# Latent attention of a decoder block: fp32 scores in row tiles of 32, in units of four heads and half the queries

## The reference, cut to what matters

```python
q = (x @ Wq.T).reshape(b, t, 16, 16).transpose(0, 2, 1, 3)
latent = layernorm(x @ Wdkv.T, ln_g, ln_b)
k = (latent @ Wuk.T).reshape(b, t, 16, 16).transpose(0, 2, 1, 3)
v = (latent @ Wuv.T).reshape(b, t, 16, 16).transpose(0, 2, 1, 3)
q = apply_rope(q); k = apply_rope(k)
scores = jnp.einsum('bhqd,bhkd->bhqk', q, k) / np.sqrt(16)
scores = jnp.where(causal, scores, -jnp.inf)
attn = jax.nn.softmax(scores, axis=-1)
out = jnp.einsum('bhqk,bhkd->bhqd', attn, v)
```

## Time and profile before

| | |
|---|---|
| median of 3 runs | 2898.22 us (2896.65 to 2900.44) |
| profiled execution | 2899.45 us, its span 2897.6 us |
| PE busy | 2651.6 us, 92% |
| DVE busy | 1506.8 us, 52% |
| ACT busy | 1233.8 us, 43% |
| POOL busy | 337.4 us, 12% |
| mean granted TensorE clock | 0.967 |

### The profile page before, as it was taken

How to read it: one execution, slowest core, us unless ns; L and a number is a source line. 1 busy time by engine, 2 the same in 40 slices (tenths; PEclk the granted TensorE clock), 3 DMA queues, 4 the chain that set the end, 5 groups by cost and what they waited for, 6 DMA issues and landing times.

```text
span 2897.6 us, 43591 instructions
## 1 busy us (share of the span) xinstructions
PE 2651.6 (92%) x14862; PEld 1626.2 (56%) x14863; DVE 1506.8 (52%) x3738; ACT 1233.8 (43%) x2620; POOL 337.4 (12%) x561
## 2 busy tenths in 40 slices
PE   7999997999999997999999987989999988987998
PEld 4565654445656544445656544445556554446997
DVE  3434468754333568744333568743443568743443
ACT  3444225653443325654443325644442425641221
POOL 1000013012000013012000022012000022013111
PEclk9999999999999999999999999999999999998999
DMA  2000000001000000001000000001000000032111
GB/s 93 12 12 1 15 1 1 1 13 41 12 11 1 15 1 1 1 13 41 17 6 1 15 1 1 0 13 46 12 6 1 15 1 1 0 124 87 55 54 39
DMA packets 32394, 56.38 MB, mean 19 GB/s; under 512 B 7108, under 2 KB 23570, under 8 KB 31858
## 3 DMA queue, kind: packets, MB, share of 16 engines
q1 hardware_dynamic: 27490, 41.33, 4.5%
q0 software_dynamic: 4752, 13.02, 1.2%
HBM read 40.01 MB, written 14.32 MB: 19 GB/s over the span
## 4 chain that ended last, share of the span: by engine, by line
PE 77%; DVE 12%; ACT 5%; issue 3%; POOL 2%; DMA 0%; SPq 0%; DVEq 0%; ACTq 0%; POOLq 0%
PE ps L939 9%; PE ps L911 8%; PE ps L884 8%; PE ps L869 5%; PE ps L929 5%; PE ps L1168 4%; PE ps L1258 4%; PE ps L1153 4%; PE ps L1272 4%; PE ps L894 4%; DVE arena L1526 3%; PE ps L1128 3%; PE ps L1031 3%; PE ps L824 3%; PE ps L1049 2%
## 5 line engine op out<-in xcount | busy, mean ns | idle before, releaser
L1360 DVE TENSOR_REDUCE neg_max<-ps 128x1 f32<-128x128 f32 (+7 forms) x256 | 194.0, 758 | 567.6 <-PE ps L914 567.3
L1526 DVE TENSOR_REDUCE arena<-ps 128x1 f32<-128x512 f32 (+3 forms) x768 | 376.4, 549 | 109.3 <-PE ps L1131 51.9
L774 ACT ACTIVATE arena<-ps 128x512 f32<-128x512 f32 (+3 forms) x768 | 320.3, 513 | 157.4 <-PE ps L1156 152.5
L939 PE MATMUL ps<-arena 128*128 128x512 f32 (+3 forms) x768 | 318.0, 501 | 4.6 <-ACT arena L660 0.5
L660 ACT ACTIVATE arena<-ps 128x512 f32<-128x512 f32 (+3 forms) x384 | 188.2, 490 | 295.3 <-PE ps L929 293.2
L1128 PE MATMUL ps<-arena 128*128 (+4 forms) x768 | 249.2, 335 | 52.1 <-DVE arena L1526 50.2
L911 PE MATMUL ps<-arena 128*128 128x512 f32 (+3 forms) x768 | 290.7, 490 | 4.4 <-ACT arena L669 4.4
L1153 PE MATMUL ps<-arena 128*128 (+4 forms) x768 | 245.0, 329 | 11.9 <-ACT arena L759 2.8
L884 PE MATMUL ps<-turned_t,arena 128*128 128x512 f32 x512 | 228.8, 600 | 1.1 <-ACT turned_t L631 1.1
L911 PEld LDWEIGHTS ps<-arena 128*128 128x128 f32 x768 | 139.1, 190 | 135.3 <-issue 114.8
L929 PE MATMUL ps<-ident,arena 128*128 128x128 f32 x1152 | 193.0, 278 | 20.8 <-ACT arena L648 11.4
(11 more groups left out here) (231 smaller groups left out, 4246.8 us busy)
## 6 DMA issues: line engine op xcount, KB each, us to landing
arena<-in_w_qkv SPq DMA_DIRECT2D x32, 384.0 KB, 3.1
arena<-in_w SPq DMA_DIRECT2D x2, 4096.0 KB, 16.8
xin<-in_x SPq DMA_DIRECT2D x5, 1024.0 KB, 5.2
xres_ids<-sorted_res SPq DMA_DIRECT2D x35, 129.0 KB, 2.1
xin<-sorted_rows SPq DMA_DIRECT2D x35, 128.0 KB, 2.0
w_out<-in_w_out SPq DMA_DIRECT2D x1, 1024.0 KB
out<-xin,out_row POOLq DMA_INDIRECT x35, 2.7
sorted_res<-xin SPq DMA_DIRECT2D x4, 129.0 KB, 2.2
```

The lines of the kernel that those rows point to most:

```text
L774: nc.scalar.activation(mprobs_t[kb % 2][:, j, lo:hi], ps[:, 3 + use % 3, 0:hi - lo], ACT.Exp).then_inc(mexp_done, 1)
L939: nc.tensor.matmul(ps[:, 6 + g, lo:BANK], v_rows[par][:, kb, :], probs_t[u % 4][:, lo:BANK], start=(kb == 0), stop=True, skip_group_check= ...
L1360: nc.vector.tensor_reduce(neg_max[:, par, t:t + 1], ps[:, buf:buf + 2, :].rearrange("p a n -> p (a n)")[:, 0:n], AX.X, ALU.max, negate=Tru ...
L1526: nc.vector.tensor_reduce(max_part[:, j, t, c:c + 1], ps[:, u % 3, 0:n], AX.X, ALU.max).then_inc(ms_taken, 1)
```

## The change

It replaces everything from the turned stacks to the products.

- q and k stay fp32. The rope writes them into `q_slots` and `k_slots`, 32 numbers per head: number 0 is 0 for a query and -1 for a key, 1 to 16 are the values, the rest 0. GpSimd fills the constants by five memsets. TensorE turns four heads at once (`turn_slots`, 8 uses of 4 transposes for q, before the latents are turned, and 8 for k), ScalarE stores all 16 halves. No stacks are made, and the keep-warm matmuls of the stage are gone.
- A score is one fp32 matmul of 32 rows of the contraction: head j of a group lies in partitions 32 j to 32 j + 31 (row tiles). No matmul adds a mask.
- The maximum of a chunk on the diagonal is taken by one VectorE instruction that adds the mask and reduces (`tensor_tensor_reduce`), 128 of 192 chunks of a batch; the others keep `tensor_reduce`. The maximum goes into slot number 0, is turned (fp32), and VectorE adds it into `q_heads_t` (`take_max`).
- ScalarE takes the exponentials of two heads in one instruction. GpSimd sets the part above the diagonal to zero afterwards (`affine_select`, 32 a batch), and products of diagonal items wait for it. Values are read from `mv_rows` directly. There are four buffers of exponentials of half the queries each.
- The work of a batch is 8 units of (group of heads, half of the queries), in the order `UNITS`; a unit of the first half has 4 items (key tiles) and 16 chunks of maxima, one of the second half 8 items and 32 chunks. While the items of a unit run, the chunks of the next are issued, 6 ahead, evenly over the items. The first unit's chunks use 7 banks, the others 3.
- The statistics for the next batch are taken on VectorE in the middle (after `take_max(5)`), the normalised rows after the last maximum. SyncE waits for `mout_taken` where it waited for `vg_ready`.

```diff
-MAX_CHUNKS = [(j, t, c) for j in range(GROUP) for t in range(NT) for c in range(t // 4 + 1)]
+UNITS = [(0, 0), (0, 1), (1, 0), (1, 1), (2, 0), (2, 1), (3, 1), (3, 0)]
+LEAD, TURN_LEAD, TAKE_LEAD = 6, 3, 4
+def max_chunk_of(s):
+    u = unit_of(FIRST_CHUNK, s)
+    (g, c), i = UNITS[u], s - FIRST_CHUNK[u]
+    if c == 0:
+        return g, (i - LEAD + 2) % GROUP, i // GROUP, 0
+    return g, (i - LEAD + 2) % GROUP, HALF + i // (2 * GROUP), (i // GROUP) % 2
+bank = m % 7 if m < FIRST_CHUNK[1] else m % 3
...
 # TensorE
-    last = nc.tensor.matmul(ps[:, u % 3, 0:n], q_stack_t[:, head, t * P:(t + 1) * P],
-                            k_stack_t[:, head, c * BANK:c * BANK + n], start=True, stop=True)
-    if diag:
-        last = nc.tensor.matmul(ps[:, u % 3, n - P:n], ident_b[:], causal_b[:], start=False, stop=True, ...)
+    rows_j = slice(SLOT * j, SLOT * (j + 1))
+    nc.tensor.matmul(ps[:, MAX_BANK[m], 0:n], q_heads_t[rows_j, g, t * P:(t + 1) * P],
+                     k_heads_t[rows_j, g, c * BANK:c * BANK + n], start=True, stop=True).then_inc(ms_done, 1)
...
+def item_scores(n, pair):
+    ...
+    if n >= 1:
+        pe.wait_ge(mexp_done, b * (2 * ITEMS) + 2 * n - 1 + pair)
+    for j in range(2 * pair, 2 * pair + 2):
+        last = nc.tensor.matmul(ps[:, 3 + j, 0:hi - lo], k_heads_t[rows_j, g, kb * P:(kb + 1) * P],
+                                q_heads_t[rows_j, g, lo:hi], start=True, stop=True)
+    last.then_inc(mst_done, 1)
...
+for n in range(ITEMS):
+    if n == FIRST_ITEM[-2]:
+        turn_max(len(UNITS) - 1)
+    item_scores(n, 0)
+    chunks(issued, chunks_by(n, 0))
+    if n >= 2:
+        item_products(n - 2)
+    item_scores(n, 1)
+    chunks(chunks_by(n, 0), chunks_by(n, 1))
+    issued = chunks_by(n, 1)
...
 # VectorE
-    nc.vector.tensor_reduce(max_part[:, j, t, c:c + 1], ps[:, u % 3, 0:n], AX.X, ALU.max).then_inc(ms_taken, 1)
+    if c < t // 4:
+        nc.vector.tensor_reduce(part, ps[:, MAX_BANK[m], 0:n], AX.X, ALU.max).then_inc(ms_taken, 1)
+    else:
+        nc.vector.tensor_tensor_reduce(max_junk[s % 2][:, 0:n], ps[:, MAX_BANK[m], 0:n], causal_wide[:, BANK - n:BANK], 1.0,
+                                       part if c == 1 else MASKED, ALU.add, ALU.max,
+                                       max_stack[:, unit_of(FIRST_CHUNK, s) % 2, t % HALF, j, 0:1]).then_inc(ms_taken, 1)
...
 # ScalarE
-    nc.scalar.activation(mprobs_t[kb % 2][:, j, lo:hi], ps[:, 3 + use % 3, 0:hi - lo], ACT.Exp).then_inc(mexp_done, 1)
+    nc.scalar.activation(mprobs_t[n % BUFS][:, 2 * pair:2 * pair + 2, lo:BANK],
+                         ps[:, bank:bank + 2, 0:BANK - lo], ACT.Exp).then_inc(mexp_done, 1)
...
 # GpSimd
+    pool.wait_ge(mexp_done, b * (2 * ITEMS) + 2 * n + 2)
+    nc.gpsimd.affine_select(mprobs_t[n % BUFS][:, :, i * P:(i + 1) * P], mprobs_t[n % BUFS][:, :, i * P:(i + 1) * P],
+                            [[0, GROUP], [1, P]], ALU.is_ge, 0.0, base=0, channel_multiplier=-1).then_inc(mdiag_done, 1)
```

More of the change, by code:

```diff
@@ L580, in _ @@
+                for u in range(len(UNITS)):
+                    if u == 5:
+                        self_scales(step, b, NORM_NEXT)
+                    keep_causal(u)
                 for h in range(2):
@@ L1095, in _ @@
                         pe.wait_ge(lat_ready, b * NT + 4 * n + t + 1)
-                        last = nc.tensor.transpose(ps[:, 4 + n, t * P:(t + 1) * P], lat_rows[:, 4 * n + t, :], ident[:])
+                        last = nc.tensor.transpose(ps[:, 6 + n, t * P:(t + 1) * P], lat_rows[:, 4 * n + t, :], ident[:])
                     last.then_inc(lat_turned, 1)
@@ new lines, in chunks @@
+                def chunks(first, end):
+                    for s in range(first, end):
+                        for u in range(len(UNITS)):
+                            if s == turn_at(u, TURN_LEAD):
+                                turn_max(u)
+                        max_chunk(s)
+                def item_scores(n, pair):
+                    u, g, c, kb = item_of(n)
+                    lo = max(kb * P, c * BANK)
+                    hi = (c + 1) * BANK
+                    if kb == 0 and pair == 0:
+                        pe.wait_ge(ms_taken, b * MAX_SLOTS + turn_count(u, TAKE_LEAD) + 1)
+                    if n >= 1:
+                        pe.wait_ge(mexp_done, b * (2 * ITEMS) + 2 * n - 1 + pair)
+                    for j in range(2 * pair, 2 * pair + 2):
+                        rows_j = slice(SLOT * j, SLOT * (j + 1))
+                        last = nc.tensor.matmul(ps[:, 3 + j, 0:hi - lo], k_heads_t[rows_j, g, kb * P:(kb + 1) * P],
+                                                q_heads_t[rows_j, g, lo:hi], start=True, stop=True)
+                    last.then_inc(mst_done, 1)
@@ new lines, in item_products @@
+                def item_products(n):
+                    u, g, c, kb = item_of(n)
+                    lo = max(kb - 4 * c, 0) * P
+                    if kb == 0 and n > 0:
+                        pe.wait_ge(mout_taken, b * (2 * NG) + u)
+                    if kb // 4 == c:
+                        pe.wait_ge(mdiag_done, b * (NG * NT) + HALF * u + kb % 4 + 1)
+                    pe.wait_ge(mexp_done, b * (2 * ITEMS) + 2 * n + 2)
+                    for j in range(GROUP):
+                        last = nc.tensor.matmul(ps[SLOT * j:SLOT * (j + 1), 7, lo:BANK], mv_rows[:, kb, GROUP * g + j, :],
+                                                mprobs_t[n % BUFS][:, j, lo:BANK],
+                                                start=(kb == 0), stop=True, skip_group_check=True)
+                    last.then_inc(mpv_done, 1)
@@ new lines, in _ @@
+                for use in range(2 * NG):
+                    turn_keys(use)
+                pe.wait_ge(mv_taken, b * NT + NT)
+                issued = FIRST_CHUNK[1] + LEAD
+                chunks(0, issued)
+                pe.wait_ge(kt_taken, b * (2 * NG) + 2 * NG)
+                for n in range(ITEMS):
[8 more added lines that the diff above has]
+                    issued = chunks_by(n, 1)
@@ L1215, in _ @@
+                for n in range(ITEMS - 2, ITEMS):
+                    item_products(n)
                 turn_rows(b, TURN_NEXT, self_rows)
@@ L1573, in _ @@
+                take_max(len(UNITS) - 1)
+                for h in range(2):
+                    normed_rows(b, NORM_NEXT, h, xin, self_rows, scale, rows_ready)
                 back_rows(1, minv)
```

450 lines of the change are left out of this document (172 added, 278 removed).

## The result

The changed kernel takes 3112.37 us (median of 4 runs, 3098.84 to 3115.61) against 2899.33 (2896.65 to 2900.44) for the one before on the same chip: ratio 1.0727, 95% interval 1.0694 to 1.076. It is slower by 213 us, where 64 less were forecast. The profiled execution took 3113.96.

A forecast was written before the change was run, and what follows sets the result against it. TensorE was busy 92%, VectorE set the stage of stacks; 459.9 + 3 x 23 + 3 x 18.5 + 28 + 9 = 621.4 against 637.4, 16.0 us a batch, 64 in four: 2834 us, range 2720 to 2940.

The forecast's parts named there:

- Granted clock near 1.00 from the first unit on: Sign named for the changed stage: TensorE keeps its full clock from the first unit; otherwise the half-clock rival holds.
- D: Rival: without keep-warm and with small tiles the clock falls to 1.2 GHz; whole stage at half gives 3102; chance 8%.
- Latents and key projection: Start of batch 0: turned query halves stand ahead of the latents, key projection 2.6 us later, last value copy at 444.7.
- First unit: Seven banks, VectorE-bound chunks before any scores: 11.1 us, scores of unit 0 start at 459.9.
- First-half units: Units 0, 2, 4, each item beside 8 chunks: VectorE 4.4 us an item plus 0.95 lost, 23 us a unit.
- stall of 0.95 us an item: At each array shape change for products: 2.6 us without a new chunk, 1.65 covered by three full banks, 0.95 left.
- Second-half units: Units 1, 3, 6, each item beside 2 small chunks: 2.6 us an item at 512 columns, 18.5 us a unit.
- step 6: Unit 5, 8 items beside 32 chunks: 25.2 us, plus 1.6 and 1.2 of uncovered statistics, 28 us.
- Unit 7: Last unit, 4 items without chunks, then the last select and products: 9 us.
- Rival A: Row-tile weight loads run one behind another: 0.45 us an item, 21.6 a batch, 2921 in all; chance 20%.
- B: Rival: row tiles don't run together; the stage ends at 741, 104 us later, 3314 in all; chance 4%.
- C: Rival: VectorE and ScalarE never wait; units take 128.6 us instead of 161.5, 2703 in all; chance 22% for most of it.

The follow-up runs named there:

- tiles_alone: Kernel before with runs of back-to-back fp32 matmuls on four, two, one row tile, column tiles and full size put in front; profiled execution 3135.27 us.
- chunk_rhythm2: Kernel before with 64 matmuls each on 32, 64 and 128 rows, freed by VectorE maxima, in front; at 32 rows a maximum every 0.94 us.
- seconds_first2: Changed kernel with the four second-half units first, then the first-half ones, statistics at unit 3; ratio 1.0046 to the kernel before, 2911.18 us.
- seconds runs: Changed kernel, second-half units first: statistics at unit 3 (1.0046), at unit 1 (1.0086), then full-size matmuls in the lead (1.0089), then paired products (1.0078).

## Why the prediction was wrong

**The step that failed** is the one on which all prices stood, put in the prediction as "Granted clock near 1.00 from the first unit on; else D". I took every TensorE duration at full clock and gave the other case 8%. Its reason, "after waits", was half right: the fall in the lead comes in a wait of 2.85 us, but the clock then stays at 0.50 for 60 us in which TensorE waits little. tiles_alone and chunk_rhythm2 show why: with 32 rows of the array at work, on one tile back to back or at VectorE's pace, the clock is 0.50 though the engine is busy all the time, and with 64 rows at the same pace it is 1.00. The kernel before had 128 rows in every score matmul, and no row read for the prediction tried fewer. D's sum, "the whole stage at the half", came to 67 us a batch over the forecast. In batch 0 it is 88 (709.0 for the last outputs, against 621.4), more than D had although the mean clock of the scores' span is 0.69, not 0.50: part of it is no matter of the clock, 5.5 us of it being a later start of the first scores (465.4 for 459.9). So D was right in its direction and its kind, and its 3102 beside 3112 is partly luck: a clock taken too low met a stage at full clock taken too short.

**How much is clock.** Length times clock gives 167 and 172 us for the scores of batches 0 and 1. That is an estimate of the least that they would take at full clock, since what doesn't scale with the clock is then undercounted; with 2 us from the last score to the last outputs it is 169 to 174, 7 to 12 more than my 161.5. From 465.4 the stage would end at some 634 to 639, against 637.4 before. So even at full clock the forecast gain of 16 us a batch would have been about nothing (3 less to 2 more), and the clock cost up to some 75 us in batch 0 and 48 in batch 1. seconds_first2 agrees: in its order the scores' span of batch 0 has a mean clock of 0.94, the last product starts at 641.0, and the ratio is 1.0046.

Point by point:

1. Latents and key projection: 2.6 us later than before was forecast; the last value copy came at 447.43 for my 444.7, another 2.7. In the later batches the whole delay is 2.0 to 2.7, as forecast.
2. First chunk on VectorE: 451.15 for 448.8, that is 3.7 us behind the last value copy for my 4.1: the price of keys was right.
3. First unit: 14.3 us from its first chunk to the first scores, 11.1 forecast. VectorE sat idle 2.23 and 2.01 us in it, which I had at nothing. By the plan of banks in the kernel, chunk 16 goes to the bank of chunk 15, so TensorE waits here until VectorE is through with all sixteen (its wait before 458.00), and VectorE then waits for TensorE. The clock fell inside this wait.
4. First-half units of 23 us: measured 35.8, 36.0, 39.5, most of each at 0.50. In seconds_first2 a first-half unit beside only 16 chunks takes 12.4 us at 1.00 (outputs at 600.23, 612.59, 624.95), less than my prices would give (4 x 3.15 + 1.6 = 14.2). The stall of 0.95 us an item is there at full clock, in front of the first chunk behind the products; what was too high is VectorE's work, 7.9 us in such a unit:

```profile
609.11 0.56 DVE L1531 CUSTOM_DVE_ANT_0 arena<-ps,causal_wide 128x384 f32<-128x384 f32 x1 [0.95 <-PE ps L1150]
612.10 0.69 DVE L1531 CUSTOM_DVE_ANT_0 arena<-ps,causal_wide 128x512 f32<-128x512 f32 x1 [0.85 <-PE ps L1150]
```

5. Second-half units of 18.5: 32.1 and 32.2 mostly at 0.50, and 22.6 for unit 6 at 1.00. This is the second term that was mis-sized, by 4.1 us. An item of 512 columns takes 2.9 us there (products start at 683.12, 686.04, 688.96 and 691.87) for my 2.6, and TensorE waits 0.96 us for the outputs of the unit before, which I had at nothing; where the rest goes wasn't read.
6. Unit 5: 34.8 us for 28, its first 14 at 0.50. Items beside four chunks at full clock: 29.9 us for 8 (seconds_first2, outputs at 517.05 and 546.99) against 26.8 by the prices of step 6. I priced them by VectorE; by the window of 490 to 570 TensorE is the bound.
7. Unit 7: 11.5 for 9.

Prices that held or erred to the safe side: four row tiles together 0.87 for 0.93; a masked maximum of 512 at 688 ns, one every 0.61 us, for my 0.70 a chunk; accumulator 82 ns for 100, hidden behind its neighbour; the select 635 ns for 1.0 us. Rival A is refuted by tiles_alone, and by the run at 523.80, where four heads' scores take 1.17 us together. B the same. C is refuted: VectorE waits 198 us for TensorE in front of L1526 alone, and at full clock its busy share is still 66% (seconds_first2, 490 to 570). The chances of D, A and B add up to 32% slower, not the 30% written.

**Left open.** What mix of shapes and waits lowers the clock in the stage: it falls in the units with eight chunks an item and not in those with four, apart from the dips beside the statistics, and warm matmuls didn't settle a share. 64-row chunks in the kernel itself weren't tried. No version that was run beats the kernel before; the nearest is seconds_first2 at 1.0046. The original order was not seen at full clock, so its cost stands only as the estimate above.

## What to carry to other kernels

Packing a matmul into a few rows saves nothing if those tiles aren't filled together. It can take the clock down with it, and then everything else on TensorE costs nearly double as well (here eight records of products 1.94 us for 1.06). Before moving from 128 rows to 32, ask which stretches will have one row tile at work, and read the granted clock there, not the busy share, which was 92% in both kernels. If such matmuls must go at another engine's pace, spread them thin beside other work of the array: here the order of eight units, with the place of the statistics, was worth 6.8%.

## What the runs showed of the hardware

- Matmuls on one row tile of 32 rows, back to back, ran at 1.2 GHz (0.50, 1.7 us for 512 fp32 columns) behind a stretch at 2.4 GHz; two and four row tiles in turn back to back, 64 rows at VectorE's pace, column tiles and full-size ones at 2.4. At VectorE's pace 32-row matmuls ran at 1.2 GHz singly, in pairs and in threes.
- Four row tiles of fp32 matmuls run as fast as one full-size matmul: 0.87 us a group at 512 columns, loads hidden.
- VectorE's masked maximum with its accumulator read costs 0.61 us at 512 columns in a row of them, the same as a plain maximum (0.60), and 746 ns instead of 688 for one when it takes a start value from SBUF.
- In the lead of the seconds runs, where VectorE is the bound, the lower clock cost nothing: VectorE did 18.2 us of work in the same 22 us at 0.56 and at 0.88.
